# Layer 3, self-attention: turning the probabilities as two 16-bit planes by DMA instead of by TensorE

## What is computed

```python
def _mha(q_in, kv_in, wq, bq, wk, bk, wv, bv, causal):
    q = einsum('btc,hcd->bhtd', q_in, wq) + bq   # k, v the same from kv_in
    scores = einsum('bhtd,bhsd->bhts', q, k) * d ** -0.5
    if causal: scores = where(tril, scores, -inf)
    p = softmax(scores, axis=-1)
    return einsum('bhts,bhsd->bhtd', p, v)       # heads side by side

h = _mha(_ln(x), _ln(x), ..., causal=True)       # self-attention
x = x + h @ m_proj_w + m_proj_b
h = _mha(_ln(x), x_e, ..., causal=False)         # cross-attention, x_e the context
x = x + h @ c_proj_w + c_proj_b
x = x + relu(_ln(x) @ f_w1 + f_b1) @ f_w2 + f_b2
```

## Time and profile before

| | before |
|---|---|
| median of 3 runs | 4764.19 us (4751.64 to 4764.62) |
| profiled execution | 4776.33 us, span 4774.5 us |
| mean granted TensorE clock | 0.945 |
| TensorE (matmul) busy | 4398.0 us, 92% |
| VectorE busy | 3302.2 us, 69% |
| ScalarE busy | 2751.1 us, 58% |
| GpSimd busy | 2635.9 us, 55% |
| transposing DMAs, layers 0 and 2 | 512, median 3.5 us to landing |

### The profile page before, as it was taken

One profiled execution on the slowest core, in us unless ns is written; L12 is line 12 of the kernel. 1 busy time (PEld: TensorE's weight loads), 2 busy tenths in 40 slices (PEclk: granted clock), 3 DMA queues, 4 the chain that ended last, 5 costly groups with the idle time before them and its releaser, 6 DMA issues.

```text
span 4774.5 us, 82536 instructions
## 1 busy us (share of the span) xinstructions
PE 4398.0 (92%) x28960; PEld 3068.3 (64%) x28960; DVE 3302.2 (69%) x6593; ACT 2751.1 (58%) x7946; POOL 2635.9 (55%) x4388
## 2 busy tenths in 40 slices
PE   7999999778888888889999999999999999999998
PEld 4545455455656565666666666666667778777777
DVE  6778777766676766676666666666666676666665
ACT  5767767677777777773333333333344666666664
POOL 6888878766566555554444444444454444444443
PEclk9999999877888888889999999999999999999999
DMA  5666656533333333334344344433332000000000
GB/s 153 126 123 131 126 119 128 116 61 67 61 67 66 61 65 61 66 82 102 72 78 75 76 72 79 76 71 81 73 78 65 15 22 19 15 22 19 15 18 7
DMA packets 984139, 337.48 MB, mean 71 GB/s; under 512 B 949040, under 2 KB 965680, under 8 KB 982320
## 3 DMA queue, kind: packets, MB, share of 16 engines
q1 hardware_dynamic: 983728, 332.22, 34.0%
HBM read 82.53 MB, written 14.68 MB: 20 GB/s over the span
## 4 chain that ended last, share of the span: by engine, by line
PE 70%; POOL 14%; issue 5%; DVE 5%; DMA 3%; ACT 3%; SPq 0%; POOLq 0%; ACTq 0%; DVEq 0%
PE ring L1482 48%; PE score L1411 8%; POOL e L2025 7%; PE ring L1425 4%; PE ring L1463 3%; POOL halves L2008 3%; POOL e L2022 2%; PE ring L1471 2%; DMA probs<-halves 2%; DMA planes<-halves 1%; PE ring L1422 1%; ACT e L1609 1%; PE ring L1446 1%; DVE probs L1796 1%; DVE nmax L1744 1%
## 5 line engine op out<-in xcount | busy, mean ns | idle before, releaser
L2025 POOL TENSOR_SCALAR e<-e,rsum 112x375 f32<-112x375 f32 (+1 forms) x2048 | 1220.1, 612 | 1255.1 <-DVE rsum L1768 1221.8
L1609 ACT ACTIVATE e<-score,nmax 112x375 f32<-112x375 f32 (+1 forms) x2048 | 1038.7, 534 | 402.6 <-DVE nmax L1744 399.9
L1744 DVE TENSOR_REDUCE nmax<-score 112x2 f32<-112x750 f32 (+1 forms) x1152 | 1071.9, 949 | 182.3 <-PE score L1411 179.4
L1482 PE MATMUL ring<-h,weights 128*128 128x224 f32 x3840 | 915.1, 376 | 57.8 <-DVE work L1896 42.2
L1482 PEld LDWEIGHTS ring<-h,weights 128*128 128x128 f32 x3840 | 733.5, 199 | 229.8 <-issue 103.2
L1411 PE MATMUL score<-keys,q 64*112 64x375 f32 (+2 forms) x3584 | 643.6, 499 | 143.5 <-ACT e L1609 131.1
L1796 DVE COPY probs<-planes 128x1344 uint16<-128x1344 uint16 x512 | 476.7, 932 | 180.2 <-DMA planes<-halves 174.4
L1482 PE MATMUL ring<-ctx,weights 128*128 128x375 f32 x1536 | 584.8, 504 | 0.7 <-DVE heads L1861 0.7
L1482 PE MATMUL ring<-weights,ctx 128*128 128x512 f32 (+4 forms) x1536 | 581.5, 511 | 0.1
L1411 PEld LDWEIGHTS score<-keys,q 64*112 64x112 f32 (+2 forms) x3584 | 224.3, 166 | 466.9 <-ACT e L1609 210.7
L2022 POOL TENSOR_SCALAR e<-e,rsumw 112x375 f32<-112x375 f32 (+1 forms) x1024 | 506.5, 512 | 30.1
(11 more groups left out here) (131 smaller groups left out, 5864.7 us busy)
## 6 DMA issues: line engine op xcount, KB each, us to landing
ctx<-ctx_t SPq DMA_DIRECT2D x128, 375.0 KB, 3.3
out_t<-x SPq DMA_DIRECT2D x64, 224.0 KB, 2.2
x<-out_t SPq DMA_DIRECT2D x48, 224.0 KB, 2.6
planes<-halves SPq DMA_TRANSPOSE x512, 3.5
weights<-weights SPq DMA_DIRECT2D x7, 1024.0 KB, 5.2
probs<-halves SPq DMA_TRANSPOSE x320, 2.7
x<-x_t SPq DMA_DIRECT2D x16, 224.0 KB, 3.1
weights<-weights SPq DMA_DIRECT2D x1, 3328.0 KB, 11.7
```

The source lines that it names most:

```text
L1482: ins = pe.matmul(out_, a, b_, start=n == 0, stop=n == len(parts) - 1)
L1609: ins = nc.scalar.activation(e_of(u)[:, n * width:(n + 1) * width], score_bank(u)[0:S, n * width:(n + 1) * width], ACT.Exp, bias=minus, sc ...
L1744: ins = dve.tensor_reduce(to, src, AX, ALU.max, negate=True)
L2025: ins = nc.gpsimd.tensor_scalar(mine, mine, rsum[0:S, slot(u), n:n + 1], 0.0, ALU.mult, ALU.add)
```

## The change

The self-attention of layer 3 goes over to words. `in_words` becomes true for it, so its turn jobs and their copies go, and each self pair gets two splits, both on GpSimd, one flip and one merge. A self pair has eight blocks of 112 columns per plane in place of a cross pair's six of 125: 16 blocks of 128 columns in `halves`, 1792 values per partition in `planes`. `halves` takes two such pairs, `planes` one: a self flip waits for the merges of whatever pair used any part of `planes` before. The product reads `probs` at the same place as before. Due positions move: the self `pv` from index + 2.7 to index + 4.2, layer 3's `o` row by 0.3. The planner is given costs for the new steps. At the end of layer 2 self pairs and cross pairs in words share `halves` and `planes`.

```diff
-SPLIT_BY = {0: ("GA",), 2: ("VV", "GG")}
+SPLIT_BY = {0: ("GA",), 2: ("VV", "GG"), 3: ("GG",)}
...
-        self.nth_halved = {p: i for i, p in enumerate(self.halved)}
+        self.nth_halved = {p: i for attn in ("cross", "self")
+                           for i, p in enumerate(p for p in self.halved if p.octet.attn == attn)}
...
-... (4.5, 0, 3.9, 4.3)[o.layer] if self.in_words(o) else lag + 0.5), "pv", ...
+... (4.5, 0, 3.9, 4.2)[o.layer] if self.in_words(o) else lag + 0.5), "pv", ...
...
+        if p.octet.attn == "self":
+            at = self.nth_halved[p] % 2 * 16 * P
+            return at, at + 16 * P
...
+    def planes_at(self, p):
+
+        if p.octet.attn == "self":
+            return 0, 16 * S
+        at = self.nth_halved[p] % PLANES * 4 * CHUNKS * S
+        return at, at + 4 * CHUNKS * S
+
+    def planes_before(self, p):
+
+        a, z = self.planes_at(p)
+        i = self.halved.index(p)
+        return [o for o in self.halved[max(0, i - 5):i] if self.planes_at(o)[0] < z and a < self.planes_at(o)[1]]
...
-        return o.layer in WORDS and o.attn == "cross"
+        return o.layer in WORDS and o.attn == "cross" or o.layer == 3 and o.attn == "self"
...
-        self.row(z + 4.0, z + 4.5, [("o", layer, s, 0, m, "V") for m in range(KC)])
+        self.row(z + 4.0 + 0.3 * (layer == 3), z + 4.5 + 0.3 * (layer == 3), [("o", layer, s, 0, m, "V") for m in range(KC)])
...
-                    self.add("split", (p, h), e, {"G": 0.95, "A": 0.8, "V": 0.6}[e], p.index + 1.4)
-                self.add("flip", p, "D", 3.5, p.index + 1.6)
-                self.add("merge", p, MERGE_BY, 0.9 if MERGE_BY == "V" else 1.2, p.index + 2.4)
+                    self.add("split", (p, h), e, {"G": 1.05 if own else 0.95, "A": 0.8, "V": 0.6}[e], p.index + 1.4)
+                self.add("flip", p, "D", 4.2 if own else 3.5, p.index + 1.6)
+                self.add("merge", p, MERGE_BY, 1.2 if own else 0.9, p.index + 2.4)
...
-            i = self.nth_halved[x]
-            if i >= PLANES:
-                yield "merge", self.halved[i - PLANES]
+            for p in self.planes_before(x):
+                yield "merge", p
...
+            if is_own(p.octet):
+                to = halves_of(p).rearrange("p (h r n) -> p h r n", h=2, n=P)
+                src = e[0:S, pair_slots(p), :].rearrange("p a n -> p (a n)").bitcast(U16).rearrange(
+                    "p (r n h) -> p h r n", r=8, h=2)
+                return to[:, h, :, 0:S], src[:, h, :, :]
...
-                        i = plan.nth_halved[p]
-                        if i >= PLANES:
-                            before = plan.halved[i - PLANES]
+                        for before in plan.planes_before(p):
                             wait.wait_ge(merged[plan.by[before]], nth["merge", before])
```

More of the change, by code:

```diff
@@ L243, in place_attention @@
             if p is o.pairs[-1] and len(o.pairs) == (2 if o.attn == "self" else 4):
-                self.pv_of[o] = self.job(p.index + (3.4 if o.layer == 1 else (4.5, 0, 3.9, 4.3)[o.layer] if self.in_words(o) else lag + 0.5), "pv", o.layer, o.s, o.b, o.half, PV_BY[o.layer], o)
+                self.pv_of[o] = self.job(p.index + (3.4 if o.layer == 1 else (4.5, 0, 3.9, 4.2)[o.layer] if self.in_words(o) else lag + 0.5), "pv", o.layer, o.s, o.b, o.half, PV_BY[o.layer], o)
     def halves_before(self, p):
@@ L955, in four_layers @@
         halves = sb("halves", [P, SPLITS * 4 * CHUNKS * P], U16)
-        planes = sb("planes", [P, PLANES, 4 * CHUNKS * S], U16)
+        planes = sb("planes", [P, PLANES * 4 * CHUNKS * S], U16)
         heads = sb("heads", [P, 16, N])
@@ L1147, in planes_of @@
         def planes_of(p):
-            return planes[:, plan.nth_halved[p] % PLANES, :]
+            a, z = plan.planes_at(p)
+            return planes[:, a:z]
         def merged_of(p):
             o = p.octet
-            at = p.units[0].k * CHUNKS
-            return part(probs[:, o.index % 2, :], 0, [8 * CHUNKS, S])[:, at:at + 2 * CHUNKS, :]
+            runs = 4 if is_own(o) else CHUNKS
+            at = p.units[0].k * runs
+            return part(probs[:, o.index % 2, :], 0, [8 * CHUNKS, S])[:, at:at + 2 * runs, :]
         def split(wait, p, h):
@@ L1189, in probs_of @@
             dt = BF16 if o.layer == 1 else F32
-            if o.layer == 1 and not is_own(o) or plan.in_words(o):
+            if not is_own(o) and (o.layer == 1 or plan.in_words(o)):
                 return part(probs[:, o.index % 2, :], 0, [8, CHUNKS, S], dt)[chunk_rows(o.layer, c), col, c, :width]
```

## The result

The changed kernel takes 4811.66 us, the median of four runs (4803.12 to 4813.72), against 4760.92 us for the kernel before on the same chip (4751.64 to 4764.62). The ratio is 1.0106, with a 95% interval of 1.0086 to 1.0126: 1.1% slower, where 1.1% faster was forecast. The time lies outside the predicted range, on its other side.

A forecast was written before the change was run, and what follows sets the result against it. Layer 3 was taken as bound by TensorE. Turns -52.5, their waits -22, new idle time +15 and later product +7 gave -52.5: 4724 us, carried over to 4712 us, 1.1% less; 8-in-10 range 4682 to 4768.

The forecast's parts named there:

- It is all on the path, as TensorE is the bound.: Self turns, mostly layer 3: removing 512 TensorE transposes saves their full time, 52.5 us, bounds 50.6 and 66.
- at most 3.5 can go: Between two cross scores after the first self quad: of 8.06 us at most 3.5 can go, the next exponentials being needed.
- The +15 for idle time newly open: After layer 3's first self quad: about 1 us of new TensorE idle time likely, +15 us in the sum.
- The -22 for waits removed: TensorE's waits at the self turns and product go: 0.98 plus about 0.5 us per stream, 22 us over 15 streams.
- (b): Rival: freed time stays idle, TensorE idle 3.5 to 6 us and more; half lost 4737 (0.14), nothing left 4764 (0.13).
- The splits, "hidden by room on their engines", at zero,: GpSimd's 128 new splits, 0.99 us each, 7.9 us per stream, leave it 61% busy and add no time.
- rival (a): Self path becomes the bound, next stream's cross scores wait for q2: +30 us, 4794; chance 0.16 together with (d).
- rival (c): Projections fill every gap and all streams have full clock: -80 us, 4684; chance 0.05.
- Merges, flips and planes: Self merges on VectorE 1.14 us each, hidden; flips land in 4.1 us; one plane buffer makes flip 2 wait for merge 1.
- The moved product: Second self quad's product comes 5.6 us later, nearly absorbed before the next cross scores; +7 us in the sum.
- (d): Rival: flips land after over 6 us, product 4 us later per stream, ending in rival (a); chance 0.16 together.

The follow-up runs named there:

- The half filling: Changed kernel with 5, 11 and 11 harmless small matmuls per stream put into TensorE's gaps after layer 3's first self quad: 4793.71 us, ratio 1.0072 to the kernel before.
- after_merges_eighth: Changed kernel, order unchanged, each self merge on VectorE cut to an eighth from sequence 4 on, splits whole: 4819.87 us, ratio 1.0102 to the kernel before.
- after_all_eighth: Changed kernel, order unchanged, self splits, flips and merges all cut to an eighth from sequence 4 on: 4779.35 us, ratio 1.0015 to the kernel before.
- before_exp_ahead7: Kernel before, turns kept on TensorE, planner's self exponentials cost 2.7 instead of 3.5 and look-ahead 7.0 instead of 6.0: 4671.89 us, ratio 0.9805.
- ahead7_turns_quarter: before_exp_ahead7 with one transpose in place of four per self turn: 4688.86 us, ratio 0.9835 to the kernel before.
- splits_on_vector: Changed kernel with both self splits on VectorE instead of GpSimd and the order made anew by the planner: 4797.02 us, ratio 1.0077 to the kernel before.

## Why the prediction was wrong

**The failed step is "It is all on the path, as TensorE is the bound."** The 52.5 us for the turns were about right as a duration (doubling them costs 44) and wrong as a gain (removing three quarters leaves the kernel between 0.5 us faster and 9 us slower, by the interval of 1.0009). The result is 103 us from the forecast, +51 in place of -52. Some 60 of these are turns and waits whose gain did not come, since the changed kernel with nearly free splits stands at +7 (1.0014); the other 44 are the splits. TensorE is busy for 95% of the stream, but not evenly at its own pace: between the first self quad and the second the times of its instructions are set by ScalarE's exponentials (one maximum and its exponentials between two cross scores, in a fixed order) and by GpSimd's weighing. The prediction saw that bound, in "at most 3.5 can go" of the 8.06 us between the cross scores of the earlier trace rows, and then still booked the whole of turns plus waits. In the trace of after these scores are 4.8 us apart, so 3.3 us did go there; they came back as longer stretches elsewhere: 9.84 us in place of 6.41 from the last of these scores to the second self quad, where the weighing is late and the clock low, and 46.4 in place of 42.4 from that quad to the next cross scores, where TensorE waits for nothing, has the full clock, and does work that had stood ahead of the quad before.

**The +15 for idle time newly open** was the right mechanism, at a third of its size. About 1 us was expected. 2.84 us opened before one group of scores alone: 15 x 2.84 = 43 us.

**The -22 for waits removed** did not happen. The wait for weighing before the first self turns went with them, but the cross turns now wait for theirs, for 0.98 us with short splits (the same figure is chance, the weighing is another) and for 2.89 with full ones. In all TensorE's idle time rose from 3.2 to 7.7 us per stream, which is the sign that the prediction gave for (b), "3.5 to 6 and more".

**The splits, "hidden by room on their engines", at zero,** are the second step that failed. Their duration was right: 937 ns against 0.99 us. Their price was not: about 44 us in place of nothing. The prediction divided busy time by the stream (61%) and compared with layer 2, where layer 2's splits do not stand in front of a step for which TensorE is waiting. It asked what is queued behind SP's new waits, and of GpSimd's queue only whether the chain to q2 would be late, in rival (a). The earlier trace rows had a sign for it: where TensorE's wait ends with POOL e, time put into GpSimd's queue ahead of that weighing can come out on TensorE.

**The clock** was in the sum with 0.68 us at most, inside rival (c). It is the other part of the price: some 64 us of matmuls (67.35 at 1.00 less 3.3 for the turns) take 67.36, so it has taken back the 3.3 us of busy time that the turns gave. Of these, 1.5 come with the splits (65.89 without most of them). The half filling says that a full clock alone would bring some 16 us back, not 50, since TensorE then waits where it had worked slowly.

**Merges, flips and planes** were sized and placed right. By line, from 3640 to 4740 us, the flips, the merges and the splits:

```profile
DMA to landing us min/median/max: 3.9/4.0/5.2
...
L1819 DVE COPY probs<-planes x58: 1075/1106/2289, 3654.7 to 4710.6; 128x1792 uint16<-128x1792 uint16 x58
...
L2031 POOL TENSOR_SCALAR halves<-e x116: 937/937/1767, 3648.3 to 4703.4; 112x896 uint16<-112x896 uint16 x116
```

Landings of 4.0 us against 4.1, merges of 1.11 against 1.14. They cost nothing, by after_merges_eighth and after_all_eighth.

**The moved product** comes 25.1 us after its scores (4012.97 to 4038.09), where it was 17.0: 8.1 later, not 5.6. Its last merge ends 24.0 us after the scores, at 4036.94, where the working had 22.5; the rest is the order, as the product waits for nothing. The q2 saves end at 4057.30, 2.05 us before the next cross scores, so no wait of TensorE comes of it. Rival (a), those scores late for want of q2, was nearest in its price (+30 against +51), and the stretch from the second self quad to them is even what it said, 46.4 us against 46.5. That is luck as far as the runs show: the stretch is full of other work and the scores do not wait. Whether the planner put them so late because it reckoned with a late q2 was not tried. Rival (b), freed time that stays idle, is what happened to the turns; as in its second form, "the change is nothing" is just what after_all_eighth measures, at 1.0015. No rival had the loss from the splits on top of it. (d) did not occur.

**The transposes and the clock.** With turns, about half of the streams had a clock of 1.00. Without three quarters of them nearly all have 0.98, and from before_exp_ahead7 to ahead7_turns_quarter the clock goes from 1.00 to 0.95 or 0.98. With the turns doubled the streams still have 1.00 or 0.98. The prediction had cited the Trainium skill (TensorE: Matmul & The Clock Gate, "Part 4: PE-mode transpose"), that transposes do not count as busy in the same way, which favoured rival (c). These runs do not bear it out: taking transposes away lowered the clock. They do not refute it either, since TensorE's idle time rose with each cut (3.2 to 4.7 us per stream, 2.5 to 3.3), and no run parts the two; nor does a run show whether these transposes are of the kind that the page means.

**What stays open.** The price of the splits, 3.4 us per stream, is 1.9 wait and 1.5 clock in one pair of traces; whether the clock would follow any other gap of that length was not separated. Nor was it tried to keep the splits on GpSimd but behind the cross weighing, or to shrink the flips alone.

## What to carry to other kernels

Before you book the removal of work from the busiest engine, look at the waits on both sides of that work: where the next one ends with another engine, the freed time can turn into wait, though added time would be paid nearly in full, and a twin with the work cut short in the unchanged order tells which in one run. An engine at 50% can still set the pace; what counts for a new instruction is what stands behind it in its queue, and whether the bounding engine already waits for that. And idle time on TensorE can cost a second time through the granted clock, though here, on its own, only some 16 us of it reached the total.

## What the runs showed of the hardware that was not expected

- The clock can undo nearly all of a saving in busy time. 3.3 us of transposes per stream were removed, and TensorE's busy time went only from 67.96 us on average to 67.36, as the granted clock fell to 0.93. Taking 24 matmuls per stream from before_exp_ahead7 made the busy time 1.2 us longer in the streams shown, with the clock at 0.95 in place of 1.00.
- VectorE's 16-bit copies and GpSimd's instructions do at times lengthen each other. One merge beside GpSimd's weighing (4008.08 to 4010.37) and fold (4010.33 to 4010.99) took 2.28 us, where the median is 1.106:

```profile
4009.66 2.28 DVE L1819 COPY probs<-planes 128x1792 uint16<-128x1792 uint16 x1
```

  In splits_on_vector, with VectorE's splits beside it, the weighing of a self quad took 6.15 us against 5.36, and two folds 1.66 against 1.28. The Trainium skill (SBUF — State Buffer, "SBUF: two separate sides") says that a VectorE instruction in a fast mode that uses both ports and a GpSimd one exclude each other for a whole instruction. The excesses (1.17 us for the merge, 0.79 us over 16 weighings) fit that, though no run shows in which mode these copies ran. The medians show how seldom it bites: 937 ns is minimum and median of 116 splits, with 1767 the longest. In after_merges_eighth, where one side of it is all but gone, no time came back.
